# Weighted sums of an attention with value halves side by side in the stationary operand, and their sum made by VectorE and GpSimd

## The reference, cut to what matters

```python
cq = rms_norm(x @ w_qa.T, q_a_ln_w)                    # latent queries, 192
q_nope, q_pe = split(cq @ w_qb.T)                      # per head 128 + 64
q_pe = q_pe * cos + rotate_half(q_pe) * sin
ckv = x @ w_kva.T
k_pe = ckv[..., 64:] ; k_pe = k_pe * cos + rotate_half(k_pe) * sin
ckv_l = rms_norm(ckv[..., :64], kv_a_ln_w)             # keys and values, 64
attn = softmax(causal(q_full @ k_full.T * scale))
out = attn @ v                                         # v = ckv_l @ w_v, per head
return out @ w_o.T
```

## Time and profile before

| what | us |
|---|---|
| median of 3 runs | 2017.91 (2014.12 to 2018.92) |
| profiled execution | 2014.93 |
| its span | 2013.1 |
| TensorE busy | 1869.8 (93%) |
| VectorE busy | 1512.2 (75%) |
| ScalarE busy | 1053.5 (52%) |
| GpSimd busy | 839.4 (42%) |

### The profile page before, as it was taken

The page is one execution under the profiler, slowest core; times in us unless marked ns, Lnnn a source line. Parts: engine busy times, 40 slices in busy tenths (PEclk is TensorE's granted clock), DMA queues, the critical chain, the costliest instruction groups (busy, mean ns, idle before and its releaser), DMA issues. The chain is left out here.

```text
span 2013.1 us, 36114 instructions
## 1 busy us (share of the span) xinstructions
PE 1869.8 (93%) x12240; PEld 1675.0 (83%) x12240; DVE 1512.2 (75%) x4199; ACT 1053.5 (52%) x2692; POOL 839.4 (42%) x865
## 2 busy tenths in 40 slices
PE   7999999999999979999899999999999999977981
PEld 6788888888888868888589999999999999977980
DVE  8978778787877755565477888888888888865756
ACT  5434333333433323333277777777777777735863
POOL 2232323233232320000044466666666666754776
PEclk9999999999999989999799999999999999998996
DMA  3201000010100104473100010000000000126877
GB/s 126 84 1 33 22 11 22 11 32 1 32 7 16 62 31 140 150 263 116 39 12 17 17 41 27 21 21 20 19 18 19 19 19 14 39 78 170 197 140 254
DMA packets 101927, 118.79 MB, mean 59 GB/s; under 512 B 12552, under 2 KB 93644, under 8 KB 101105
## 3 DMA queue, kind: packets, MB, share of 16 engines
q1 hardware_dynamic: 89024, 108.35, 16.8%
q0 software_dynamic: 12288, 8.11, 2.7%
q10 hardware_dynamic: 432, 0.02, 0.0%
HBM read 75.43 MB, written 57.10 MB: 66 GB/s over the span
## 5 line engine op out<-in xcount | busy, mean ns | idle before, releaser
L237 POOL TENSOR_TENSOR rwkv_gate<-rwkv_key,rwkv_gate 128x512 f32<-128x512 f32 x128 | 203.9, 1593 | 524.0 <-DVE rwkv_key L442 524.0
L1429 POOL TENSOR_TENSOR kept_raw<-kept_raw,mla_row_inv 128x512 f32<-128x512 f32 x192 | 199.7, 1040 | 265.2 <-DVE mla_row_inv L1780 264.6
L310 ACT ACTIVATE rwkv_gate<-rwkv_r 128x512 f32<-128x512 f32 x128 | 76.9, 600 | 400.3 <-DVE rwkv_o_low L363 397.8
L1588 ACT ACTIVATE kept_raw<-kept_raw,mla_least 128x256 f32<-128x256 f32 (+1 forms) x512 | 228.7, 449 | 79.1 <-DVE mla_least L1764 77.6
L1764 DVE CUSTOM_DVE_ANT_0 kept_raw<-mla_score,kept_mask 128x256 f32<-128x256 f32 (+1 forms) x512 | 156.9, 353 | 83.1 <-PE mla_score L2137 53.1
L427 DVE TENSOR_TENSOR rwkv_kv<-rwkv_v,rwkv_key 128x512 f32<-128x512 f32 x128 | 88.1, 688 | 123.9 <-PE rwkv_v L475 120.8
L434 DVE TENSOR_TENSOR_SCAN rwkv_state<-rwkv_decay_w,rwkv_kv 128x256 f32<-128x256 f32 x256 | 166.4, 692 | 4.1
L492 PE MATMUL rwkv_out<-rwkv_w_high,rwkv_o_high 128*128 128x256 f32 x512 | 144.2, 282 | 6.2 <-DVE rwkv_o_low L363 6.2
L492 PE MATMUL rwkv_out<-rwkv_w_high,rwkv_o_low 128*128 128x256 f32 x512 | 145.1, 283 | 0.0
L492 PE MATMUL rwkv_out<-rwkv_w_low,rwkv_o_high 128*128 128x256 f32 x512 | 144.2, 282 | 0.0
L1514 POOL DMA_INDIRECT slots<-mla_x_out,mla_slot_now x128 | 129.6, 1012 | 31.0 <-issue 23.7
(11 more groups left out here) (400 smaller groups left out, 6275.6 us busy)
## 6 DMA issues: line engine op xcount, KB each, us to landing
kept_raw<-in_experts SPq DMA_DIRECT2D x27, 384.0 KB
kept_raw<-in_rkvo SPq DMA_DIRECT2D x16, 512.0 KB
moe_y_in<-sums SPq DMA_DIRECT2D x32, 256.0 KB, 4.6
sums<-ffn_empty SPq DMA_DIRECT2D x12, 512.0 KB
slots<-ffn_empty SPq DMA_DIRECT2D x16, 361.2 KB
moe_e_rows<-slots SPq DMA_DIRECT2D x32, 180.6 KB
kept_x_in<-x SPq DMA_DIRECT2D x18, 256.0 KB, 16.3
mla_x_res<-x SPq DMA_DIRECT2D x17, 256.0 KB
```

What stands on the lines that cost most here:

```text
L237: nc.gpsimd.tensor_tensor(gate[:, c % 2, :], key[:, c % 2, :], gate[:, c % 2, :], ALU.mult).then_inc(gated_done, 1)
L1429: nc.gpsimd.tensor_tensor(unit, unit, row_inv[:, v % PR, 0:len(heads)].rearrange("p (h a) -> p h a", a=1) .to_broadcast([P, len(heads), ke ...
L1588: last = nc.scalar.activation(probs[:, v % PR, i * keys:(i + 1) * keys], masked[:, v % 2, i * keys:(i + 1) * keys], ACT.Exp, bias=least[:, ...
```

## The change

The high and the low part of the values stand side by side in one stationary operand of 128 columns (v_parts), and each of the two parts of the probabilities streams past it with 512 columns: 2 matmuls for 128 keys, 4 for 256. Partitions 0 to 63 of the bank hold the sum with the high values, 64 to 127 that with the low values, for all four heads; the product low by low is now in it. ScalarE copies the lower half to SBUF (keep_low_sums, in slot v + 5), VectorE adds it to the upper one in two instructions of 64 partitions, which also put even heads in partitions 0 to 63 of o_whole and odd heads in 64 to 127 (add_sums, slot v + 5). A slot later ScalarE makes the high part from o_whole (sums_high) and GpSimd the low part (sums_low, at the end of its slot). o_whole and low_sum have two buffers. The bank is free when the additions are done (o_added); project_out still waits for o_low. The zeros beside the values are gone. The rotations of queries and keys take their sine part in one instruction in place of two, and the router's steps 21 and 26 are tensor_tensor against constant tiles.

```diff
@@ -1127,7 +1127,7 @@
...
-        v_part = both("v", [P, 2, 2, 2, 2 * KVL])
+        v_parts = s.sb("v", [P, 2, 2, 2 * KVL], F32R)
@@ -1137,6 +1137,8 @@
...
+        low_sum = s.sb("low_sum", [KVL, 2, 512])
+        o_whole = s.sb("o_whole", [P, 2, 2, P])
@@ -1296,8 +1301,7 @@
...
             group = group_of(seq, v)
             tile, j = group // 4 % 2, group % 4
-            return (group, o_ps[j % 2][:, 0:SEQ].rearrange("p (a q) -> p a q", q=P),
-                    (slice(None), tile, slice(2 * j, 2 * j + 2), slice(None)))
+            return group, o_ps[j % 2], (slice(None), tile, slice(2 * j, 2 * j + 2), slice(None))
@@ -1430,6 +1430,12 @@
...
+            def sums_low(seq, v):
+                group, _, where = sums_of(seq, v)
+                pool.wait_ge(o_high, group + 1)
+                nc.gpsimd.tensor_tensor(o_part[1][where], o_whole[:, group % 2, :, :], o_part[0][where].bitcast(F32),
+                                        ALU.subtract).then_inc(o_low, 1)
@@ -1468,6 +1474,9 @@
...
+                m, of, vs = slot_before(seq, v, SUM_LAG + 2)
+                if m >= 0 and completes(vs):
+                    sums_low(of, vs)
@@ -1570,13 +1579,9 @@
...
             def values_high(seq, par):
...
-                act.wait_ge(v_zeroed, 1)
...
-                for b in range(2):
-                    last = nc.scalar.activation(v_part[0][:, par, :, b, b * KVL:(b + 1) * KVL],
-                                                k_rows[:, :, 0:KVL], ACT.Copy)
-                last.then_inc(v_high, 1)
+                nc.scalar.activation(v_parts[:, par, :, 0:KVL], k_rows[:, :, 0:KVL], ACT.Copy).then_inc(v_high, 1)
@@ -1591,10 +1596,17 @@
...
+            def keep_low_sums(seq, v):
+                group, bank, _ = sums_of(seq, v)
+                act.wait_ge(summed, group + 1)
+                if group >= 2:
+                    act.wait_ge(o_added, group - 1)
+                nc.scalar.activation(low_sum[:, group % 2, :], bank[KVL:, :], ACT.Copy).then_inc(low_kept, 1)
+
             def sums_high(seq, v):
-                group, src, where = sums_of(seq, v)
-                act.wait_ge(summed, group + 1)
-                nc.scalar.activation(o_part[0][where], src, ACT.Copy).then_inc(o_high, 1)
+                group, _, where = sums_of(seq, v)
+                act.wait_ge(o_added, group + 1)
+                nc.scalar.activation(o_part[0][where], o_whole[:, group % 2, :, :], ACT.Copy).then_inc(o_high, 1)
@@ -1635,9 +1647,12 @@
                 m, of, vt = slot_before(seq, v, TURN_LAG)
                 if m >= 0:
                     probs_high(m, vt)
+                m, of, vs = slot_before(seq, v, SUM_LAG + 2)
+                if m >= 0 and completes(vs):
+                    sums_high(of, vs)
                 m, of, vs = slot_before(seq, v, SUM_LAG + 1)
                 if m >= 0 and completes(vs):
-                    sums_high(of, vs)
+                    keep_low_sums(of, vs)
@@ -1721,23 +1736,18 @@
...
-                for a in range(2):
-                    b = at + (1 - a) * (DR // 2)
-                    last = nc.vector.tensor_tensor(k_turn[:, t, 1, a * (DR // 2):(a + 1) * (DR // 2)],
-                                                   ps[:, b:b + DR // 2],
-                                                   rk[:, 1, t, a * (DR // 2):(a + 1) * (DR // 2)], ALU.mult)
-                last.then_inc(lat_scaled, 1)
+                nc.vector.tensor_tensor(k_turn[:, t, 1, :].rearrange("p (a d) -> p a d", a=2),
+                                        ps[:, at:at + DR].rearrange("p (a d) -> p a d", a=2)[:, ::-1, :],
+                                        rk[:, 1, t, :].rearrange("p (a d) -> p a d", a=2), ALU.mult)\
+                    .then_inc(lat_scaled, 1)
...
                 dve.wait_ge(v_high, seq + 1)
-                for b in range(2):
-                    half = slice(b * KVL, (b + 1) * KVL)
-                    last = nc.vector.tensor_tensor(v_part[1][:, par, :, b, half], k_rows[:, :, 0:KVL],
-                                                   v_part[0][:, par, :, b, half].bitcast(F32), ALU.subtract)
-                last.then_inc(v_low, 1)
+                nc.vector.tensor_tensor(v_parts[:, par, :, KVL:], k_rows[:, :, 0:KVL],
+                                        v_parts[:, par, :, 0:KVL].bitcast(F32), ALU.subtract).then_inc(v_low, 1)
@@ -1747,12 +1757,10 @@
...
-                for a in range(2):
-                    half = slice(a * (DR // 2), (a + 1) * (DR // 2))
-                    last = nc.vector.tensor_tensor(
-                        q_sin[:, c, :].rearrange("p (h d) -> p h d", d=DR)[:, :, half], q[:, :, 1 - a, :],
-                        rq[:, 1, tile:tile + 1, half].to_broadcast([P, 8, DR // 2]), ALU.mult)
-                last.then_inc(q_turned, 1)
+                nc.vector.tensor_tensor(
+                    q_sin[:, c, :].rearrange("p (h a d) -> p h a d", a=2, d=DR // 2), q[:, :, ::-1, :],
+                    rq[:, 1, tile:tile + 1, :].rearrange("p o (a d) -> p o a d", a=2)
+                    .to_broadcast([P, 8, 2, DR // 2]), ALU.mult).then_inc(q_turned, 1)
@@ -1779,11 +1787,17 @@
...
-            def sums_low(seq, v):
-                group, src, where = sums_of(seq, v)
-                dve.wait_ge(o_high, group + 1)
-                nc.vector.tensor_tensor(o_part[1][where], src, o_part[0][where].bitcast(F32), ALU.subtract)\
-                    .then_inc(o_low, 1)
+            def add_sums(seq, v):
+                group, bank, _ = sums_of(seq, v)
+                dve.wait_ge(low_kept, group + 1)
+                if group >= 2:
+                    dve.wait_ge(o_low, group - 1)
+                high = bank[0:KVL, :].rearrange("p (a b q) -> p a b q", a=2, b=2)
+                low = low_sum[:, group % 2, :].rearrange("p (a b q) -> p a b q", a=2, b=2)
+                for b in range(2):
+                    last = nc.vector.tensor_tensor(o_whole[b * KVL:(b + 1) * KVL, group % 2, :, :], high[:, :, b, :],
+                                                   low[:, :, b, :], ALU.add)
+                last.then_inc(o_added, 1)
@@ -1880,7 +1894,7 @@
...
                 elif step == 21:
-                    v.tensor_scalar(weight_sum[:, :], weight_sum[:, :], 1e-20, None, ALU.add).then_inc(chain, 1)
+                    v.tensor_tensor(weight_sum[:, :], weight_sum[:, :], least_sum[:, :], ALU.add).then_inc(chain, 1)
@@ -1894,7 +1908,7 @@
...
                 elif step == 26:
-                    v.tensor_scalar(full[:, :, :], place_k[:, :, :], float(CAP), None, ALU.is_ge)\
+                    v.tensor_tensor(full[:, :, :], place_k[:, :, :], most_places[:, :, :], ALU.is_ge)\
@@ -1950,7 +1966,7 @@
...
                 m, of, vs = slot_before(seq, v, SUM_LAG + 1)
                 if m >= 0 and completes(vs):
-                    sums_low(of, vs)
+                    add_sums(of, vs)
@@ -2149,19 +2165,20 @@
             def weighted_sums(seq, v):
...
-                group, out, _ = sums_of(seq, v)
+                group, bank, _ = sums_of(seq, v)
...
                 if group >= 2:
-                    pe.wait_ge(o_low, group - 1)
-                terms = [(b, kb, vp, pp) for kb in range(keys // P) for b in range(2) for vp, pp in PARTS]
-                for i, (b, kb, vp, pp) in enumerate(terms):
+                    pe.wait_ge(o_added, group - 1)
+                terms = [(kb, pp) for kb in range(keys // P) for pp in range(2)]
+                for i, (kb, pp) in enumerate(terms):
                     if tile == 0:
-                        probs_t = p_part[pp][:, v % PR, :].rearrange("p (a b q) -> p a b q", b=2, q=P)[:, :, b, :]
+                        probs_t = p_part[pp][:, v % PR, :]
                     else:
-                        probs_t = p_part[pp][:, (v - 1) % PR:v % PR + 1, (2 * b + kb) * P:(2 * b + kb + 1) * P]
-                    last = nc.tensor.matmul(out, v_part[vp][:, seq % 2, kb, b, :], probs_t, start=(i == 0),
+                        probs_t = p_part[pp][:, (v - 1) % PR:v % PR + 1, :]\
+                            .rearrange("p a (b k q) -> p a b k q", b=2, k=2)[:, :, :, kb, :]
+                    last = nc.tensor.matmul(bank[:, :], v_parts[:, seq % 2, kb, :], probs_t, start=(i == 0),
                                             stop=(i == len(terms) - 1))
                 last.then_inc(summed, 1)
...
```

13 lines of the change are left out of this document (7 added, 6 removed).

## The result

The changed kernel takes 2067.98 us (median of 4 runs, 2060.82 to 2073.32) beside 2018.41 for the kernel before in the same comparison: 1.0247 times as long, 95% interval 1.0222 to 1.0273. The forecast was 2036, at most 2050. Slower was right, the size was not: + 50 us instead of + 18. The profiled execution has a span of 2063.6 us against 2013.1.

What follows compares the result with a forecast made beforehand. TensorE looked like the bound (97.66 busy), with GpSimd's queue unresting up to y0. Terms -6.5, +18.7 (11 x 1.7) and +6 sum to +18.2 on 2017.91, forecasting 2036 us; range 2008 to 2050.

Steps and rivals of the forecast that it cites:

- The prices: Expected instruction times: 512-column matmuls 0.235 apart, o_low 0.73, ScalarE's copies 0.595 and 0.38, VectorE's two additions 0.76 at most.
- The chain up to y0: GpSimd's queue from slot 3 to y0 in sequences with scatters: y0 at 28.1 instead of 25.69, +2.4 us.
- before the change the two have nothing to do with each other: Slot 9's scatter ending on GpSimd and y0 starting on TensorE coincide at 1336.32, unconnected until the change.
- from y0 to the next slot 3: - 0.7: TensorE's slot 1 saving (0.5) and half a router step (0.25) arrive, ScalarE takes part: -0.7, bounds -0.4 and -1.0.
- The half-way gain: First of two router steps rewritten as tensor_tensor on VectorE: half of a possible 0.47 us saving counted, 0.25.
- The first three sequences: Sequences 0 to 2, without scatters: TensorE's saving mostly arrives, 1.5 plus 2.5 for each of two, -6.5 us.
- The last two: Sequences 14 and 15, without latents ahead of y0: y0 waits for GpSimd, +3 each, +6 us.
- some 4: Expected wait in us before y0 in sequences 14 and 15: six o_low (4.2) less GpSimd's rests.
- The loop through slot 6: Rival: VectorE's wait in slot 6 grows into a loop, +3.0 to +4.0 a sequence, 2050 to 2061 us; chance 0.08.
- The change cancels out: Rival: every term at its lower bound, 0 a sequence, 2006 to 2022 us, likeliest 2014; chance 0.2.
- TensorE's 47 us are won: Rival: TensorE's whole matmul saving arrives, 1971 us at best, 1990 with 1.2 a sequence lost; chance 0.12.
- no rest from slot 7 to y0: GpSimd's queue before the change works without a wait from slot 7 (1325.12) to slot 9's scatter end (1336.32).

Runs made afterwards that it cites:

- 12 to 14: Three kernels with scatters moved to earlier slots: changed, additions and o_low cut, 2002.20 us; kernel before with new rotations, 2018.35; changed, additions cut, 2021.76.
- 4: Changed kernel plus 14 unread matmuls of 256 columns on TensorE in slot 10, ahead of its wait for the latents: 2060.66 us, ratio 1.0229.
- 6: Changed kernel with GpSimd's o_low subtraction cut from 256 elements to 2: 2022.72 us, ratio 1.0036.
- 10: Changed kernel with both VectorE's additions and GpSimd's o_low cut to 2 elements: 2015.96 us, ratio 1.0001.
- 7: Changed kernel with GpSimd's eight scatters in slots 1, 2, 2, 3, 4, 5, 6, 7 instead of 2 to 9: 2031.59 us, ratio 1.0076.
- 5: Kernel before plus a spare 128x256 subtraction on GpSimd in eight slots a sequence, for which nobody waits: 2046.23 us, ratio 1.0150.
- 9: Changed kernel with VectorE's two additions cut from 256 elements to 2 each, o_low at full size: 2065.22 us, ratio 1.0244.
- 3: Changed kernel with GpSimd's o_low ahead of the scatter and router's steps of the same slot instead of behind: 2059.47 us, ratio 1.0224.
- 12: Changed kernel with additions and o_low cut to 2 elements and scatters in slots 1, 2, 2, 3, 4, 5, 6, 7: 2002.20 us, ratio 0.9936.
- 2: Changed kernel with o_low moved back from GpSimd to VectorE: 2037.22 us, ratio 1.0115.

## Why the prediction was right about the sign and wrong about the size

**The prices were right.** The matmuls of 512 columns start 0.23 apart; ScalarE's copies and VectorE's additions and values are at or near their forecast; o_low took 0.74 (forecast 0.73). In ns, min/median/max:

```profile
L1437 POOL TENSOR_TENSOR mla_o_low<-mla_o_whole,mla_o_high x128: 722/740/910, 1037.8 to 1821.5; 128x256 fp32r<-128x256 f32 x128
...
L1798 DVE TENSOR_TENSOR mla_o_whole<-mla_o,mla_low_sum x256: 353/417/421, 1034.0 to 1817.9; 64x256 f32<-64x256 f32 x128
...
L1604 ACT ACTIVATE mla_low_sum<-mla_o x128: 594/595/600, 1032.6 to 1816.7; 64x512 f32<-64x512 f32 x128
```

Two additions took 0.83 together, where I had 0.76: in this form neighbours don't overlap much.

**The chain up to y0 was right to 0.1 us.** From slot 3's start at 1319.42: slots 3 to 5 end at 11.06 (forecast 11.1), slot 7's scaling begins at 14.70 (14.75), y0 at 28.17 (28.1), and VectorE waits for o_low before slot 6's additions, 0.52. y0 is released by the last o_low in every sequence from 3 on, as forecast. What I had not seen is that a second thing hangs on the same queue at the same time: the latents' rstd. TensorE's long wait (2.1) is for that one, and what is left for o_low behind it is 0.8 at most. I had listed lat_rstd among what comes later, and then followed y0 alone. Nor was it so that "before the change the two have nothing to do with each other": the rstd came just in time for the latents, right ahead of y0 (12 to 14).

**The step that failed is "from y0 to the next slot 3: - 0.7".** It measured 1319.42 - 1296.31 = 23.11 against 22.43, + 0.68; 11 times the difference of 1.4 is 15.4, and 34.1 - 18.7 is the same 15.4. Measured from y0 of sequence 5, TensorE's slots 11, 0, 1 and 3 begin 0.72, 0.64, 0.89 and 0.60 later than before the change. I had a saving of 0.7 there and put the clock at nothing.

The lowered clock is the first part: y0 lasts 3.6 instead of 2.9 us. The first scores of slot 3 stand on TensorE 19.81 behind that y0 before the change, 20.41 after it, and 19.79 in 4, where the clock stays up: 0.6.

The second part is the 0.7 that I let through and that did not arrive even at full clock. With o_low cut 0.35 of it arrives (19.46 in 6), with the additions cut as well 0.5 (19.31 in 10). The wait for p_low grew by 0.23, because TensorE comes to it earlier: VectorE's step ends 6.9 behind y0 before the change, in 4 and in 10, so nothing of slot 11's saving arrives, as I had said. The wait for place_e grew by 0.25 for another reason. Right ahead of place_e VectorE makes the norm's two steps, and GpSimd's new o_low of slot 11 runs beside the first of them. The pair takes 0.99 instead of 0.74 us (rows 1 and 2: before, after). Without o_low, in 6, it is 0.73 and the wait is 0.2 (rows 3 and 4); in 7, with o_low, it is 0.99 again and the wait 0.5 (row 5).

```profile
1343.71 0.74 DVE L1816 TENSOR_SCALAR mla_x_out<-mla_y_rows,mla_moments,mla_rstd 128x256 f32<-128x256 f32 x2
...
1355.63 0.99 DVE L1830 TENSOR_SCALAR mla_x_out<-mla_y_rows,mla_moments,mla_rstd 128x256 f32<-128x256 f32 x2
...
1342.28 0.73 DVE L1832 TENSOR_SCALAR mla_x_out<-mla_y_rows,mla_moments,mla_rstd 128x256 f32<-128x256 f32 x2
...
PE mla_turn L2127 <- DVE mla_place_e L1848: 2.6, 11, 0.2
...
PE mla_turn L2126 <- DVE mla_place_e L1847: 5.5, 11, 0.5
```

The router gave nothing back either. The two steps written as tensor_tensor did not get shorter (the first two rows below), and a third, which had been short in the earlier trace rows, became long (row 3), because GpSimd's new o_low of slot 1 runs beside it. Row 4 is this third step in run 5, where only GpSimd's spare subtraction was added, row 5 in run 6, where o_low was cut, row 6 in run 7, where the moved scatters shift o_low away from it: long in the first, short in the other two. In 7 the wait for place_e is as long as in the changed kernel, so no run shows that this third step costs TensorE anything.

```profile
L1897 DVE TENSOR_TENSOR mla_weight_sum<-mla_weight_sum,mla_least_sum x16: 161/632/637, 1149.4 to 1856.4; 128x2 f32<-128x2 f32 x16
...
L1911 DVE TENSOR_TENSOR mla_full<-mla_place_k,mla_most_places x16: 166/650/655, 1157.7 to 1859.6; 128x8 f32<-128x8 f32 x16
...
L1914 DVE SCALAR_TENSOR_TENSOR mla_slot_f<-mla_best_at,mla_place_k x16: 166/649/654, 1158.3 to 1859.8; 128x8 f32<-128x8 uint32 x16
...
L1909 DVE SCALAR_TENSOR_TENSOR mla_slot_f<-mla_best_at,mla_place_k x16: 167/662/666, 1162.5 to 1841.7; 128x8 f32<-128x8 uint32 x16
...
L1916 DVE SCALAR_TENSOR_TENSOR mla_slot_f<-mla_best_at,mla_place_k x16: 166/168/170, 1156.9 to 1815.8; 128x8 f32<-128x8 uint32 x16
...
L1915 DVE SCALAR_TENSOR_TENSOR mla_slot_f<-mla_best_at,mla_place_k x16: 166/167/169, 1158.8 to 1825.9; 128x8 f32<-128x8 uint32 x16
```

The half-way gain I took was nothing. The first two rows fit the rule of the Trainium skill (SBUF — State Buffer, Who interferes with whom) that I had weighed against it: a tensor_tensor whose inputs both lie in SBUF contends with GpSimd's reads.

**The first three sequences: - 1.3 instead of - 6.5.** There GpSimd has no scatters, and I let 2.5 of TensorE's 2.9 through, and 1.5 in sequence 0. 0.7 and 0.8 came, and in sequence 0 nothing (+ 0.2). Even with additions and o_low both cut it was 1.2 and 1.1 (10). Where the rest goes isn't settled: behind y0 of sequence 0 slot 1 begins after 10.0 us in both kernels, so the saving of slot 11 does not get past slot 0, and another 0.4 goes before slot 8.

**The last two: + 19.6 instead of + 6.** The waits of 4.14 and 3.98 are the "some 4" of the working. I took only 3 each from them, forgot y1 of sequence 15, which waits 5.69 (0.93 before), and did not count that y0 runs at half clock behind each: 24 matmuls 0.21 apart take 5.3 instead of 2.9 us.

**The rivals.** That VectorE's queue sets the pace is excluded for the changed kernel by 9. The loop through slot 6 (2050 to 2061) did not come about, though the time lies beyond it: the chain through slot 6 took what was forecast. "The change cancels out" needed a chain up to y0 that was not longer, and it was 2.5 longer. "TensorE's 47 us are won" needed six o_low to cost nothing; in 6 and 10 they cost little, and the period still was 48.32 and 47.97. The cut subtractions take 0.21 each, six of them some 1.2 up to y0, so without any the period might be near 46.8 (an estimate; no run has it), which is 1.3 of TensorE's 2.9. I had the sentence ("no rest from slot 7 to y0") and used it only for what is added, not for what TensorE could gain.

What 5, 4 and the changed kernel say of the 3.14 us a period: GpSimd's added time 1.8, the lowered clock 0.5, and 0.9 for the rest of the change, which includes everything that TensorE saved. The parts are differences between different kernels, and what the 0.9 is made of no single run shows.

## To carry to other kernels

When an engine's queue shows no rest, list everything that it delivers in that stretch and who waits for each, not only the new product: the limit is the latest of them, and a wait that was removed while its twin stayed bought nothing in the period (3). Before counting a saving on the busiest engine, look for a second queue of the same length. Here it hardly showed as a wait (0.09 at most), only in the distance from the rstd to the latents, which was the same 1.22 in every sequence; it held the period at 48.0 when the added work was cut (10), and moving work that had nothing to do with the change let 1.2 of the saving through (12). And a wait of some 2 us on TensorE cost more than its length here, because the matmuls behind it ran at the lower clock in 9 of 11 sequences.

## What the runs showed of the hardware

- TensorE's clock was granted at 0.50 behind an idle of 2.08 us in a kernel that was otherwise busy, and stayed up with 14 useless matmuls in that idle (0.41 left): periods of 50.7 instead of 51.3 to 51.5. In two sequences of eleven the same idle did not lower it, and idle times of 1.6 us (5) and 1.3 us (2) in the same place left it at 1.00 in all eleven.
- A subtraction on GpSimd that nobody waits for (5) slowed a step of 8 elements on VectorE, with all operands in SBUF, from 168 to 662 ns in the median. It depends on what falls beside what: in 7, with a subtraction of the same size a little earlier or later, the step took 167.
- GpSimd took 1228 ns for a tensor_scalar of 128x256 with two operands per partition, against 740 for its subtraction of the same size: the form with fewer full operands is the dearer one here.
